# One PSUM bank for the gram, three for the transposes, in a recommendation-tower kernel

## The reference, cut to what matters

```python
e = jnp.stack([tbl_0[ids[:, 0]], ..., tbl_25[ids[:, 25]]], axis=1)
combined = jnp.concatenate([dense[:, None, :], e], axis=1)           # (2048, 27, 128)
interactions = jnp.einsum('bfd,bgd->bfg', combined, combined)[:, _IU0, _IU1]
z = jnp.concatenate([dense, interactions], axis=1)
h = jnp.maximum(jnp.concatenate([z, dense], axis=1) @ W_top1 + b_top1, 0.0)   # 512
h = jnp.maximum(h @ W_top2 + b_top2, 0.0)                                      # 256
y = h @ W_top3
```

## Time and profile before

| | |
|---|---|
| median of 3 executions | 545.93 us |
| lowest, highest | 544.96, 546.94 us |
| the profiled execution | 544.32 us |
| its span, first to last instruction | 542.2 us |
| mean granted TensorE clock | 0.865 |
| ACT busy | 164.0 us, 30% |
| DVE busy | 208.5 us, 38% |
| gram matmuls (L390) | 2048, 84.0 us busy |
| select matmuls (L368) | 1152, 335.9 us busy |

### The profile page before, as it was taken

One profiled execution on the slowest core, in us unless ns is written; L12 is line 12 of the kernel. 1 busy time (PEld: TensorE's weight loads), 2 busy tenths in 40 slices (PEclk: granted clock), 3 DMA queues, 4 the chain that ended last, 5 costly groups with the idle time before them and its releaser, 6 DMA issues.

```text
span 542.2 us, 9738 instructions
## 1 busy us (share of the span) xinstructions
PE 397.3 (73%) x3968; PEld 350.2 (65%) x3968; DVE 208.5 (38%) x156; ACT 164.0 (30%) x314; POOL 258.2 (48%) x278
## 2 busy tenths in 40 slices
PE   0700767476783898769885798768985988879997
PEld 0600666375672697658774697557864887769887
DVE  5702965115141362236331362414433173338112
ACT  1200442232331243324330243313422143425330
POOL 6774456646465245655556255543546435530000
PEclk9965789688895799979995789958998689979999
DMA  8921551574131062415332142313413131212021
GB/s 229 276 61 28 160 173 40 137 157 121 38 69 52 23 140 57 77 39 117 97 65 54 39 126 56 76 34 70 123 39 80 34 78 44 60 31 53 2 52 31
DMA packets 66211, 43.88 MB, mean 81 GB/s; under 512 B 51697, under 2 KB 56392, under 8 KB 66060
## 3 DMA queue, kind: packets, MB, share of 16 engines
q1 hardware_dynamic: 55924, 25.48, 19.4%
q0 software_dynamic: 8704, 17.84, 12.9%
q10 hardware_dynamic: 1560, 0.24, 0.3%
HBM read 37.78 MB, written 5.76 MB: 80 GB/s over the span
## 4 chain that ended last, share of the span: by engine, by line
PE 47%; another core or an unknown queue 21%; issue 15%; DVE 10%; ACT 3%; DMA 2%; ACTq 0%; SPq 0%; DVEq 0%
PE p_sel L368 25%; PE p_gram L390 10%; DVE onehot L657 5%; PE p_turn L349 4%; PE p_mlp L411 3%; PE p_mlp L448 2%; DVE p_gram L627 2%; DVE low L636 2%; ACT feats L555 2%; PE p_mlp L460 1%; PE p_mlp L405 1%; DMA prods<-in_table 1%; ACT feats L534 1%; DMA square<-prods 1%
## 5 line engine op out<-in xcount | busy, mean ns | idle before, releaser
L321 POOL DMA_INDIRECT rows<-in_table,index x272 | 257.6, 947 | 221.0 <-PE p_turn L349 116.1
L657 DVE TENSOR_TENSOR onehot<-ids_all,p_rows 128x2048 fp32r<-128x2048 int32 x72 | 163.2, 2283 | 175.1 <-PE p_sel L368 104.0
L368 PE MATMUL p_sel<-onehot,high 125*128 125x256 f32 x576 | 170.6, 325 | 78.4 <-DVE low L636 40.7
L368 PEld LDWEIGHTS p_sel<-onehot,high 125*128 125x128 f32 x576 | 127.6, 222 | 87.6 <-issue 86.9
L368 PE MATMUL p_sel<-onehot,low 125*128 125x256 f32 x576 | 165.3, 316 | 6.0 <-issue 5.8
L368 PEld LDWEIGHTS p_sel<-onehot,low 125*128 125x128 f32 x576 | 128.3, 223 | 10.7 <-issue 10.3
L390 PE MATMUL p_gram<-feats 128*54 128x52 f32 x2048 | 84.0, 230 | 46.5 <-issue 41.3
L390 PEld LDWEIGHTS p_gram<-feats 128*54 128x54 f32 x2048 | 71.0, 144 | 66.1 <-issue 61.6
L534 ACT ACTIVATE feats<-p_turn 128x512 f32<-128x512 f32 (+1 forms) x80 | 79.7, 1002 | 59.3 <-remote 36.8
L570 ACT ACTIVATE prods<-p_gram 118x416 f32<-118x416 f32 x64 | 33.3, 520 | 160.3 <-remote 115.3
L555 ACT ACTIVATE feats<-p_sel 128x128 f32<-128x128 f32 x144 | 45.8, 443 | 109.3 <-remote 52.5
(11 more groups left out here) (29 smaller groups left out, 77.7 us busy)
## 6 DMA issues: line engine op xcount, KB each, us to landing
ids_all<-in_ids_t SPq DMA_DIRECT2D x25, 256.0 KB, 4.4
square<-prods SPq DMA_DIRECT2D x62, 87.8 KB
rows<-in_table,index POOLq DMA_INDIRECT x272
prods<-in_table SPq DMA_DIRECT2D x9, 448.0 KB
pairs<-square SPq DMA_DIRECT2D x14, 117.0 KB
ids_all<-in_ids_t SPq DMA_DIRECT2D x1, 1152.0 KB
dense<-in_x_t SPq DMA_DIRECT2D x1, 896.0 KB
ids_all<-in_ids_t SPq DMA_DIRECT2D x6, 128.0 KB
```

The lines of the kernel that those rows point to most:

```text
L321: pool.indirect_dma_start(out=rows[a][:, f, :], out_offset=None, in_=tables[f], in_offset=bass.IndirectOffsetOnAxis(ap=index[:, (2 * i + a ...
L368: mm = pe.matmul(p_sel[k % 2][:, 0:PAIR], part[k][0:VP, c, :], hot, start=(c == 0 and part is high), stop=(c == VC - 1 and part is low))
L657: nc.vector.tensor_tensor(onehot[k % RING][:, :, :], at, of, ALU.is_equal).then_inc(s_onehot, 1)
```

## The change

`p_gram` becomes a single bank, and the other bank of the pair becomes a third `p_turn`. Each gram bank now waits for the copy of the one before it. In the loop and in pair 7 s1 moves from behind g3 to between g2 and g3, and the later selects are dealt out anew (two behind turn2, two behind turn3, three behind turn4), so that turn2, turn3 and turn4 come one select earlier. In pair 1 the four gram banks are spread over turn0 and turn1. A turn waits for the last copy out of its own bank (`turn_free`); pairs 0 and 1 keep to two banks for the turns of their first tiles. The gram of the last tile stays in one piece.

```diff
+TURNS = (0, 1, 2, 0, 1, 2, 0, 1, 2, 1)
+HEAD_TURNS = (0, 1) * NQ
+def turn_free(slot, first, second):
+    n = 2 * NQ + slot
+    banks = (HEAD_TURNS if first or second else TURNS) + (HEAD_TURNS if first else TURNS)
+    return n - max((k for k in range(n) if banks[k] == banks[n]), default=NQ)
...
 def selections(q, first, second):
...
-    n, early = NQ, EARLY if second else 1
-    if not second:
-        q, n = q - 1, n - 1
-        if q < 0:
-            return range(0)
-    return range(early + q * (SEL - early) // n, early + (q + 1) * (SEL - early) // n)
+    start = 1 if second else 2
+    q, n = q - start, NQ - start
+    if q < 0:
+        return range(0)
+    return range(EARLY + q * (SEL - EARLY) // n, EARLY + (q + 1) * (SEL - EARLY) // n)
...
-        p_turn = [ps(f"p_turn{k}") for k in range(2)]
-        p_pair = ctx.enter_context(nc.psum_tensor("p_gram", [128, 2, 512], F32))
-        p_gram = [p_pair[:, k, :] for k in range(2)]
+        p_pair = ctx.enter_context(nc.psum_tensor("p_pair", [128, 2, 512], F32))
+        p_turn = [ps(f"p_turn{k}") for k in range(2)] + [p_pair[:, 0, :]]
+        p_gram = p_pair[:, 1, :]
...
             def turn(i, a, q, first=False, second=False):
-                    pe.wait_ge(s_feats, n - 1)
+                    pe.wait_ge(s_feats, n + 1 - turn_free(NQ * a + q, first, second))
...
             def gram(i, a, banks):
-                    if not (isinstance(n, int) and n < 2):
-                        pe.wait_ge(s_prods, n - 1)
+                    if not (isinstance(n, int) and n < 1):
+                        pe.wait_ge(s_prods, n)
...
             def pair(i, first=False, second=False, last=False):
                 if second:
-                    gram(0, 1, range(NG))
+                    gram(0, 1, (0,))
                 for q in range(NQ):
...
-                    turn(i, 0, q, first)
+                    turn(i, 0, q, first, second)
+                    if second and q < 2:
+                        gram(0, 1, (1,) if q == 0 else (2, 3))
                     if q < 2 and not (first or second):
-                        gram(i - 1, 1, range(NH * q, NH * q + (NH + 1) // 2))
-                        if q == 0:
-                            select(i, 0)
-                        gram(i - 1, 1, range(NH * q + (NH + 1) // 2, NH * q + NH))
+                        gram(i - 1, 1, (2 * q,))
+                        select(i, q)
+                        gram(i - 1, 1, (2 * q + 1,))
...
         # ACT
                 if second:
-                    keep_prods(0, 1, range(NG), first=True)
+                    keep_prods(0, 1, (0,), first=True)
...
-                    if second and q == 0:
+                    if second and q < 2:
+                        keep_prods(0, 1, (1,) if q == 0 else (2, 3), first=True)
+                    if q == 1 and not first:
                         for k in range(EARLY):
                             keep_selected(i, k)
-                    if q == 1 and not (first or second):
-                        keep_selected(i, 0)
```

More of the change, by code:

```diff
@@ L142, in bank1 @@
         def bank1(m, tail):
-            return (p_turn + p_sel)[m] if tail else p_mlp
+            return (p_turn[:2] + p_sel)[m] if tail else p_mlp
         def bank2(m, tail):
-            return p_gram[m] if tail else p_mlp
+            return (p_gram, p_turn[2])[m] if tail else p_mlp
         s_zero = sem("s_zero")
@@ L338, in _, with turn @@
         def _(pe):
-            def turn(i, a, q, first=False):
+            def turn(i, a, q, first=False, second=False):
                 n = NQ * (2 * i + a) + q
@@ L345, in turn @@
                 if not (first and a == 0 and q < 2):
-                    pe.wait_ge(s_feats, n - 1)
+                    pe.wait_ge(s_feats, n + 1 - turn_free(NQ * a + q, first, second))
+                bank = p_turn[(HEAD_TURNS if first else TURNS)[NQ * a + q]]
                 for k, f in enumerate(quad):
-                    mm = pe.transpose(p_turn[(NQ * a + q) % 2][:, k * T:k * T + T], rows[a][:, f, :],
+                    mm = pe.transpose(bank[:, k * T:k * T + T], rows[a][:, f, :],
                                       ident[:, :])
@@ L389, in gram @@
                             group = feats[a][:, GB * b + k, js, :].rearrange("d j f -> d (j f)")
-                            mm = pe.matmul(p_gram[b % 2][WIDE * tile:WIDE * tile + BLK, BLKC * k:BLKC * k + BLKC], group,
+                            mm = pe.matmul(p_gram[WIDE * tile:WIDE * tile + BLK, BLKC * k:BLKC * k + BLKC], group,
                                            feats[a][:, GB * b + k, js, 1:C], start=True, stop=True)
@@ L487, in pair @@
                 for q in range(NQ):
-                    turn(i, 1, q, first)
+                    turn(i, 1, q, first, second)
                     if q < 2:
@@ L532, in keep @@
                 dst = feats[a][:, :, :, 1 + quad[0]:1 + quad[-1] + 1].rearrange("d g j f -> d f j g")
-                src = p_turn[(NQ * a + q) % 2][:, 0:len(quad) * T].rearrange("d (f j g) -> d f j g", j=4, g=GS)
+                bank = p_turn[(HEAD_TURNS if first else TURNS)[NQ * a + q]]
+                src = bank[:, 0:len(quad) * T].rearrange("d (f j g) -> d f j g", j=4, g=GS)
                 nc.scalar.activation(dst, src, ACT.Copy).then_inc(s_feats, 1)
@@ L568, in keep_prods @@
                     act.wait_ge(s_gram, NG * t + b + 1)
-                    src = p_gram[b % 2][0:RISE, 0:GB * BLKC].rearrange("p (g c) -> p c g", g=GB)
+                    src = p_gram[0:RISE, 0:GB * BLKC].rearrange("p (g c) -> p c g", g=GB)
                     nc.scalar.activation(prods[a][0:RISE, :, GB * b:GB * b + GB], src, ACT.Copy)\
```

## The result

| | before | after |
|---|---|---|
| median, four executions each | 545.44 us | 577.99 us |
| lowest, highest | 544.80, 546.94 | 574.74, 579.12 |
| ratio, 95% interval | | 1.058 (1.053 to 1.063) |
| the profiled execution, its span | 544.32, 542.2 | 577.23, 575.1 |
| mean granted TensorE clock | 0.865 | 0.834 |

The change costs 32.5 us. The prediction said slower, by 4.2 us, and its range ended at 557. In the kernel after, the gram bank is called p_pair and its matmuls have L401; a select is L379, a turn L360, `keep_prods` L583, `keep_selected` L568, the gather L331.

The account below looks back on a forecast made before the run. The prediction took the loop to be bound by PE completion reports held back while POOL issues gathers. Its terms summed to +4.2 us on a median of 545.93, forecasting 550.1 us, range 542 to 557.

Parts of the forecast that it names:

- the step that carries most of it: Layer 1 blocks: g1's wait for g0's copy is hidden by PE's window stall; uncovered, it costs 0.55 us a time.
- Layer 1: Five first blocks of tile 1's turns: earlier gathers save 1.0 us each, -5.0 us, bounds 0 and -6.2.
- Before s2: Loop, turn1 to s2: s2 stays 7.8 us after turn1; turn2 gains 1.8 us over four pairs, pair 3 loses 4.0.
- g2 keeps its place, so its report should too: Loop, behind turn1: g2 is reported before the window bites, so g3's new wait for its copy costs nothing.
- slower rival: Loop: g2's report is held back too, s2 starts 1.5 us later five times, +7.5, 557.6 us; chance 0.17.
- The selects: Behind s2 in the loop: more selects end within gather windows, 0.5 us each pair, +2.5 us.
- The top of the loop: Start of a loop pair: g1 waits for g0's copy, +0.7 us in each of three pairs, +2.1 us.
- Pairs 0 and 1: Copy waits in pair 0, +0.4 us; pair 1's gram spread out, -1 us with bounds -4 and +5.
- Pair 7 and the tail: Pair 7: a gap before s2, +0.8 us; last tile's gram: three banks wait for copies, +2.2 us.
- Nothing moves in the loop: Third rival: gather windows pace the loop in any order; only pair 7 and tail count, +3.0, 548.9 us; chance 0.14.
- A single bank is free: Last rival: the copies hide everywhere, three terms of 5.1 us vanish, 545.0 us; chance 0.07.
- The third bank for the transposes: Turns in the loop: gains nothing, since no turn there waits for a copy.

Follow-up runs that it names:

- after_again: The changed kernel, unchanged, run again beside the kernel before: 576.76 us, ratio 1.065 to the kernel before.
- two_banks_tile0: The changed kernel with two transpose banks and two gram banks for tile 0's gram only, between the layer 1 blocks: 563.37 us, ratio 1.037 to the kernel before.
- one_bank_old_order: The kernel before with one gram bank, order unchanged: 551.79 us, ratio 1.038; repeated later: 570.18 us (1.061), and 389.99 us (1.031) with prompt reports.
- second group: Runs on one chip: both kernels unchanged again, plus two variants of the changed kernel; the kernel before took 547.17 us.
- before_again: The kernel before, unchanged, run again as a kernel of its own: 544.97 us, ratio 0.989 to itself.
- order_only: The changed kernel's new order with the two gram banks and two transpose banks of the kernel before: 541.77 us, ratio 1.021 to the kernel before.
- one_bank_two_turns: The changed kernel without the third transpose bank, still one gram bank: 575.72 us, ratio 1.063 to the kernel before.
- plain_loads: The kernel before with each gather of pairs 1 to 7 replaced by a plain load of 128 table rows, with prompt reports: 380.47 us.
- early_turns: The kernel before with turn2 to turn4 one select earlier and pair 1's gram spread; two gram banks, old g2, g3, s1: 560.47 us, ratio 1.040.
- before_third: The kernel before, unchanged, run again in a group with prompt reports: 381.91 us, one execution.

## Why the prediction was wrong in size

**Right: what bounds the kernel in the executions it read.** The loop is paced by late reports: without the gathers 131 us go. But the prediction took the lateness for a property of the gathers. It needs something else too: 545 and 380 us are the same kernel with the same gathers.

**Wrong, the step that carries most of it: "but PE already stands until the window's end with g1 half issued, so this is hidden by that stall. If that cover is gone it costs 0.55 us a time."** Layer 1 was forecast at -5.0 us and measured at +13.2 (3.7 and 9.5), and two banks in that place alone bring 13.4 us back. The stall was real, but the step took what lay in it for free. With two banks the stall holds 20 to 28 matmuls of the next bank, and a report at the window's end releases only the rest of them; with one bank it releases the copy (0.52), all 32 matmuls (1.0 to 1.2) and then the turn. What is uncovered is not the copy, but the copy and a bank: 1.6 us a block (9.2 on average in after_again, 7.6 in two_banks_tile0), ten blocks in the loop. The figure of 0.55 was the price for a copy reported at once. The step also read the slot of the report from the execution at hand, and that slot moves: at W + 4.2 the forecast "hidden" is right (one_bank_old_order, blocks unchanged), at W + 5.7 it is not. The profile that the prediction read had W + 4.2 in all second blocks, and that of after has W + 5.7 in all of them. That part of the miss could not be read from one execution.

**Layers 2 and 3** had no term and lost 9.1 us (6.5 in the second group), 7.7 of them in pairs 2 and 3, by a late report of layer 2 that was not there before. two_banks_tile0 has none of it, so it follows from the stalls in the blocks. The prediction asked which wait ends last in a stage that it changed, but not whether a later turn drags its gathers over a stage that it left alone.

**Before s2.** Forecast: g2's report comes at T + 1.4, s2 at T + 7.8, in pair 3 another 0.85 later (+2.9). Measured T + 8.8, 8.8, 8.8, 8.1 and 9.4 (+6.9). The premise "g2 keeps its place, so its report should too" failed: in pairs 2, 3, 4 and 6 g2 itself starts 1.1 to 1.7 us late, since it has to wait for the copy of g1, a wait that has no term in the sum, and then ends inside the window. This is the slower rival's mechanism (chance 0.17: s2 at T + 9.3), and the loop came near it in four of the five pairs. That rival as a whole, 557.6, missed by 20 us all the same, as it had the same layer 1 terms.

**The selects.** Forecast +1.9 with turn2 and the clock counted in, measured +9.2. Between s2 and the first turn of tile 1 PE stands 8.7 us in the five pairs of after, nearly all of it for the copies of selects, and 0.7 us in those of before. That is the wait that the prediction named, at 0.5 us a pair; the upper end of its 0.4 to 1.9 would have been +9.5. But the total of such waits in the whole run is the same in both (15.2 and 15.5 us), and before_again stands 10.1 us in this stretch, with the old order: in the second group the stretch grows by 0.6 us only. So the +9.2 is a low value of before as much as a cost of the change.

**The first layer 1 block.** The gain of the earlier turns is real (order_only, 8.6 to 7.4), and in the change the single bank takes it back and more.

**The top of the loop.** Forecast +2.1, measured -16.9. In pair 4, before, the chain of this stretch is full of pauses of PE; these are three of them:

```profile
286.75 1.18 issue
...
288.89 1.16 issue
...
291.08 1.06 issue
```

The same stretch of after has this one and one of 0.48:

```profile
302.15 1.47 issue
```

All pauses in that stretch sum to 5.5 us before and 1.95 after, and that is most of what turn0 to T gains in this pair (16.3 to 10.6). I read it as work that is late anyway finding POOL further on; no run isolates it. The other stages of the loop lose 38.4 us, and this one gives 16.9 of them back. In the second group it gives back 1.3 of 29.7. So most of this gain belongs to the execution of before in the result, and not to the change.

**Pairs 0 and 1.** Forecast -0.6, measured +6.2, of which 2.75 lie in the start-up and 3.4 are in the bounds given.

**Pair 7 and the tail.** Forecast +0.8 and +2.2. In the runs without late reports pair 7 costs 1.27: the forecast gap of 1.2 less 0.44 is there (0.77), but the two banks take 1.01 and 0.96 apart instead of 1.74 together, and s1 alone 2.10. In the profile of after it is 2.9, the rest of it ahead of T. The tail is 2.45, near the forecast. "Nothing moves in the loop", the third rival, counted these two alone, 3.0; the bare cost of the change is 1.27 in each of six pairs and 2.45 in the tail, 10 us.

**A single bank is free.** This rival fell in every run. What speaks for it in the Trainium skill, "TensorE: Matmul & The Clock Gate", section "HAM oscillation", is one matmul kernel to which PSUM double-buffering gave no further gain. It doesn't carry over to this kernel: one bank for two costs 9.6 and 11.7 us of 380 where reports are prompt, and 3.8% and 6.1% where they are late.

**The third bank for the transposes** gains nothing, as forecast (one_bank_two_turns).

**What stays open.** Why the groups differ, and whether it is the chip at all; whether it is the issuing or the transfers of the gathers that hold reports back where they do (plain_loads ran where nothing is late); and what decides between W + 4.2 and W + 5.7. Some 13 of the 30 us of the second group are shown to hang on the bank between the layer 1 blocks; how the rest splits between the order and the single bank of tile 1 is not. The halves don't add up either: one bank 1.038 and 1.061, the order 1.021 and, as early_turns, 1.040, both 1.058 and 1.065, with a kernel before that moves by 1% against itself.

## What to carry to other kernels

Before one of two buffers is taken away, don't price the wait as it is drawn on paper (copy plus release, 0.6 us) but by the report in the trace: the consumer's start less the producer's end. If that distance is ever several us, a second buffer is what lets the engine work through it, and what has been done in such a stall counts as hidden work that the change uncovers. And a cover read from one execution holds for that execution's report times: a change that moves a kernel by a few per cent should be profiled more than once, and in more than one session.

## What the hardware did that I had not expected

- One kernel, two speeds: 545, 538, 547 and 541 us in some groups, 380 and 378 us in others, with the same 945 ns per gather issued. The trace tells them apart at a glance: PE busy 73% against 89%, and the copy of a gram bank starting up to several us behind its matmuls (4.7 in pair 4) against 0.11 at most in before_third.
- Held back reports of the gram come mostly in steps, counted from the start of a window of four gathers: near 1.3, 2.8, 4.2 and 5.7 us in before, nearly all at 2.8 and 5.7 in after. The gathers themselves start every 1.25 us. A bank that is full at W + 1.9 is reported in the same slot nearly throughout an execution: at 4.2 in all seven cases of before and all eleven of order_only, at 5.7 in all seven of before_again and all nine of after.
- Where reports are late the kernel before ranges from 526 to 557 us over four groups, while after stays within 574.7 to 579.1 in its eight executions of two groups. Why wasn't looked into.
